# Closer-spaced last norms, one feed-forward step per event, and a norm's scale and shift folded into the output product

## The reference, cut to what matters

```python
# second attention block, on x = layernorm(h)
combined = mh_out + kv_ret                     # two retrievals from running sums
mu = combined.mean(-1, keepdims=True)
var = combined.var(-1, keepdims=True)
lnx = (combined - mu) / jnp.sqrt(var + 1e-05) * ln_g + ln_b
return x + (lnx @ out_w + out_b)
# second feed-forward block, on features = layernorm(h); 6 experts, the best 2 are kept
rh = jax.nn.relu(features @ router_w1 + router_b1)
expert_logits = jax.nn.softmax(rh @ router_w2 + router_b2, axis=-1)
top_w, top_i = jax.lax.top_k(expert_logits, TOP_K)
routing_weights = jax.nn.softmax(top_w, axis=-1)
h1 = jax.nn.relu(jnp.einsum('bsd,edh->bseh', features, expert_w1) + expert_b1)
h2 = jax.nn.relu(jnp.einsum('bseh,ehf->bsef', h1, expert_w2) + expert_b2)
expert_out = jnp.einsum('bsef,efo->bseo', h2, expert_w3) + expert_b3
# the chosen two, weighted and added
```

## Time and profile before

| | us |
|---|---|
| median of 3 runs | 1428.61 |
| lowest and highest | 1426.0, 1433.91 |
| the profiled execution, own time | 1428.26 |
| its span, first to last instruction | 1426.3 |

### The profile page before, as it was taken

The page is one execution under the profiler, slowest core; times in us unless marked ns, Lnnn a source line. Parts: engine busy times, 40 slices in busy tenths (PEclk is TensorE's granted clock), DMA queues, the critical chain, the costliest instruction groups (busy, mean ns, idle before and its releaser), DMA issues.

```text
span 1426.3 us, 26246 instructions
## 1 busy us (share of the span) xinstructions
PE 1163.8 (82%) x9789; PEld 741.6 (52%) x9789; DVE 810.9 (57%) x1763; ACT 643.1 (45%) x1370; POOL 552.9 (39%) x1126
## 2 busy tenths in 40 slices
PE   4599999999999999999999963603287865785688
PEld 3355666656666666666666642201265654653443
DVE  3445555655566566565666522225798989835432
ACT  0326555555554555555455421301546546443444
POOL 3201445734545545455454443178512224212100
PEclk9769999999999999999999986955676777677889
DMA  3100000000000000000000011112000000000000
GB/s 81 20 1 2 2 2 2 5 5 2 4 2 2 2 2 2 2 2 2 2 3 2 2 30 60 62 16 21 7 1 1 1 1 1 12 1 6 11 11 17
DMA packets 31290, 14.59 MB, mean 10 GB/s; under 512 B 27570, under 2 KB 28562, under 8 KB 31165
## 3 DMA queue, kind: packets, MB, share of 16 engines
q1 hardware_dynamic: 26557, 11.01, 3.2%
q0 software_dynamic: 4608, 1.91, 1.5%
HBM read 6.52 MB, written 7.27 MB: 10 GB/s over the span
## 4 chain that ended last, share of the span: by engine, by line
PE 74%; DVE 15%; issue 4%; POOL 2%; ACT 2%; DMA 2%; SPq 0%; DVEq 0%; POOLq 0%; ACTq 0%
PE psum L753 20%; PE psum L734 10%; PE psum L662 8%; PE psum L725 7%; PE psum L709 3%; PE psum L1001 3%; PE psum L647 2%; PE psum L981 2%; PE psum L572 1%; DVE arena L1971 1%; PE psum L991 1%; PE psum L1016 1%; PE psum L667 1%; PE psum L850 1%; PE psum L804 1%
## 5 line engine op out<-in xcount | busy, mean ns | idle before, releaser
L1436 ACT ACTIVATE arena<-psum 125x500 f32<-125x500 f32 x576 | 306.8, 585 | 338.8 <-PE psum L734 338.8
L1777 DVE TENSOR_REDUCE arena<-psum 125x1 f32<-125x500 f32 x384 | 242.6, 673 | 203.1 <-PE psum L662 202.9
L662 PE MATMUL psum<-arena 32*125 32x500 f32 (+1 forms) x1536 | 324.5, 520 | 0.6 <-ACT arena L1427 0.6
L753 PE MATMUL psum<-arena,XN 125*64 125x250 f32 x2304 | 307.9, 388 | 0.2 <-ACT arena L1436 0.2
L734 PE MATMUL psum<-arena 32*125 32x250 f32 x2304 | 291.7, 370 | 0.0
L734 PEld LDWEIGHTS psum<-arena 32*125 32x125 f32 x2304 | 214.6, 183 | 11.8 <-issue 1.0
L753 PEld LDWEIGHTS psum<-arena,XN 125*64 125x64 f32 x2304 | 140.3, 136 | 121.2 <-issue 78.6
L1780 DVE TENSOR_REDUCE arena<-psum 125x2 f32<-125x500 f32 x192 | 121.4, 674 | 71.9 <-PE psum L662 71.9
L1193 POOL TENSOR_TENSOR lnst<-lnst,mhalf 125x12 f32<-125x12 f32 x14 | 32.2, 2297 | 256.9 <-DVE lnst L1756 256.9
L662 PEld LDWEIGHTS psum<-arena 32*125 32x125 f32 x1536 | 128.1, 184 | 4.1 <-issue 2.4
L725 PE MATMUL psum<-arena,onesb 3*125 3x500 bf16 x576 | 122.4, 422 | 1.4 <-DMA arena<-arena 1.4
(11 more groups left out here) (337 smaller groups left out, 1951.3 us busy)
## 6 DMA issues: line engine op xcount, KB each, us to landing
arena<-arena SPq DMA_DIRECT2D x192, 1.5 KB
expert_in<-XN SPq DMA_DIRECT2D x8, 256.0 KB, 4.8
arena<-expert_in SPq DMA_DIRECT2D x4, 512.0 KB, 5.1
expert_out<-arena SPq DMA_DIRECT2D x4, 512.0 KB, 2.6
out<-H SPq DMA_DIRECT2D x16, 93.8 KB
expert_in<-XN,slot_in POOLq DMA_INDIRECT x48, 2.5
XN<-expert_out,slot_out POOLq DMA_INDIRECT x48, 3.9
arena<-in_L_ffn_w SPq DMA_DIRECT2D x2, 256.0 KB
```

Source lines behind the costliest of these rows:

```text
L662: last = pe.matmul(ps[0:R, at_:at_ + hi - lo], QH[row:row + 32, b, g, j * R:(j + 1) * R], KH[row:row + 32, b, g, lo:hi], start=True, stop= ...
L753: last = pe.matmul(ctx_bank[64 * h2:64 * h2 + 64, 0:THIRD], XN[:, p, c, a, :], PR[:, x % 4, h2, i * THIRD:(i + 1) * THIRD], start=(c == 0) ...
L1436: act.activation(PR[:, x % 4, h2, :], st_bank[(2 * x + h2) % 3][0:R, 0:2 * THIRD], ACT.Exp)\
L1777: dve.reduce_max(MX[:, q % 2, 0, 2 * h2 + tile:2 * h2 + tile + 1], ps[0:R, 0:2 * THIRD], AX)\
```

## The change

Three things. (1) The list of events: norm and head events get a written place for each quarter (`norm_at`, `gate_at`), `gates` is split in two events (`weighed` for the DVE's `route` and ACT's last exponential; `gates` for the PE's turn and ACT's copies, one x later), and from x = 23 on each x has exactly one step. (2) `ln_g` is multiplied into the rows of `out_w` once, `ln_b @ out_w` is worked out once by a matmul and added to `out_b`, and GpSimd's two operations at `normalize` go. (3) With it, `ln_g` and `ln_b` are loaded as columns (four DMAs) where they were loaded as broadcast rows (two DMAs).

The diff, cut to its core:

```diff
-        ROOM, EARLY, PER = 16, True, 2
         steps1 = [(p, th, ep) for p in range(NP) for th in range(2) for ep in range(3)]
...
-        def ffn_events(x):
...
+        ROOM, FIRST, PER = 16, 23, 1
+        norm_at = {0: (8, 9, 10, 11, 12, 13, 14, 16), 1: (14, 15, 16, 17, 18, 19, 20, 22),
+                   2: (20, 21, 22, 23, 24, 25, 26, 28), 3: (26, 27, 28, 29, 30, 31, 32, 34)}
+        gate_at = {0: 19, 1: 23, 2: 29, 3: 35}
+        todo = [("step", k) for k in range(len(steps1) + 3)]
...
             for p in range(NP):
-                k = x - NJ * (p + 1) - 2
-                if 0 <= k <= 11 and k not in (3, 9, 10):
-                    events.append((("centre", "variance", "normalize", "", "transpose", "product",
-                                    "centre", "variance", "normalize", "", "", "transpose")[k], 2 + k // 6, p))
+                for n, name in enumerate((("centre", 2), ("variance", 2), ("normalize", 2), ("transpose", 2),
+                                          ("product", 0), ("centre", 3), ("variance", 3), ("transpose", 3))):
+                    if norm_at[p][n] == x:
+                        events.append((*name, p))
+            for p in range(NP):
+                if 0 <= x - gate_at[p] <= 3:
+                    events.append((("router", "logit", "weighed", "gates")[x - gate_at[p]], p))
...
-            if EARLY:
-                ffn_events(x)
-        ffn_events(None)
+            for _ in range(PER if x >= FIRST else 0):
+                k = todo[0][1]
+                if x > gate_at[steps1[min(k, len(steps1) - 1)][0]] + 3:
+                    events.append(todo.pop(0))
+        events += todo
...
+                   (W["lng"][r, :], t["L1_attn_ln_g"].unsqueeze(1)),
+                   (W["lnb"][r, :], t["L1_attn_ln_b"].unsqueeze(1)),
...
             def product(p):
 
+                pe.wait_ge(S["out_scaled"], 1)
...
+            pe.wait_ge(S["shift_rows"], 1)
+            ps, done = take(pe, "out_bias")
+            pe.matmul(ps[0:R, 0:128], QF[:, 0, 0:R], W["outw"], start=True, stop=True).then_inc(done, 1)
...
-                    transposes(x, xn_tile, event[2], S["lnx"] if x == 2 else S[f"normed{x}"])
+                    transposes(x, xn_tile, event[2], S[f"normed{x}"])
...
-                pool.tensor_tensor(pairs(H, p), pairs(H, p), rows(bias[0:R, OB:OB + D], 2 * NJ), ALU.add)\
+                if p == 0:
+                    pool.wait_ge(S["out_bias"], 1)
+                pool.tensor_tensor(pairs(H, p).rearrange("r (j a) d -> r j (a d)", a=2),
+                                   pairs(H, p).rearrange("r (j a) d -> r j (a d)", a=2),
+                                   rows(bias[0:R, OBX:OBX + 128], NJ), ALU.add)\
                     .then_inc(S["h_pre"], 1)
...
-                elif kind == "normalize" and x == 2:
-
-                    p = event[2]
-                    pool.wait_ge(S["normed2"], p + 1)
-                    link(pool.tensor_tensor(pairs(XN, p), pairs(XN, p), rows(bias[0:R, LNG:LNG + D], 12), ALU.mult))
-                    pool.tensor_tensor(pairs(XN, p), pairs(XN, p), rows(bias[0:R, LNB:LNB + D], 12), ALU.add)\
-                        .then_inc(S["lnx"], 1)
...
+            act.wait_ge(S["dma_weights"], 16 * len(wd))
+            act.activation(QF[:, 0, 0:R], ones[:, 0:R], ACT.Copy, scale=W["lnb"]).then_inc(S["shift_rows"], 1)
+            k = jobs["out_bias"]
+            act.wait_ge(full[k % 8], k // 8 + 1)
+            act.activation(W["outw"], W["outw"], ACT.Copy, scale=W["lng"]).then_inc(S["out_scaled"], 1)
...
+            ps, done = filled(dve, "out_bias")
+            link(dve.tensor_tensor(bias[0:R, OBX:OBX + 128].rearrange("r (a d) -> r a d", a=2),
+                                   ps[0:R, 0:128].rearrange("r (a d) -> r a d", a=2),
+                                   rows(bias[0:R, OB:OB + D], 2), ALU.add))
...
-                elif kind == "gates":
+                elif kind == "weighed":
                     route(x)
```

More of the change, by code:

```diff
@@ L44 @@
 RS = 1.0 / np.sqrt(float(PP))
-GB, CVB, KSB, GTB, AOB, LNG, LNB, OB, RB2, WD = (
-    0, 8, 264, 392, 394, 658, 722, 786, 850, 856)
+GB, CVB, KSB, GTB, AOB, OB, RB2, WD, OBX = (
+    0, 8, 264, 392, 394, 658, 722, 728, 733)
 NBIAS = 861
@@ L259, in build @@
             "cosines", "prod", "qf_ready", "state", "h_pre", "lnx",
-            "route1", "route1_ex", "route1_pad", "select", "stored")
+            "route1", "route1_ex", "route1_pad", "select", "shift_rows", "out_bias", "out_scaled", "stored")
         gathered = [S["gathered0"], S["gathered1"], S["gathered2"], S["gathered3"]]
@@ L324, in build @@
         mx, im, pos, sums, kept, sl, sx, tx, sy = (r1[:, i, :] for i in range(9))
-        ROOM, EARLY, PER = 16, True, 2
         steps1 = [(p, th, ep) for p in range(NP) for th in range(2) for ep in range(3)]
-        head1 = [(kind, p) for p in range(NP) for kind in ("router", "logit", "gates")]
-        body1 = [("step", k) for k in range(len(steps1) + 3)]
-        given = []
-        def ffn_events(x):
[L336 to L361, removed]
+        ROOM, FIRST, PER = 16, 23, 1
[3 more added lines that the diff above has]
+        todo = [("step", k) for k in range(len(steps1) + 3)]
         events = [("gathered", 0), ("centre", 1, 0), ("variance", 1, 0), ("gathered", 1), ("centre", 1, 1),
@@ L366, in build @@
                   ("cosines", 0), ("chunk", 0)]
-        for x in range(NT + 14):
+        for x in range(NT + 16):
             p, k = divmod(x, NJ)
@@ L547, in build @@
                 wd.append((bias[:, at_:at_ + n], t["L1_attn_" + name].partition_broadcast(128)))
-        for at_, name, n in ((GB, "L0_ffn_gate_b", 8), (LNG, "L1_attn_ln_g", 64), (LNB, "L1_attn_ln_b", 64),
-                             (OB, "L1_attn_out_b", 64), (RB2, "L1_ffn_router_b2", 6)):
+        for at_, name, n in ((GB, "L0_ffn_gate_b", 8), (OB, "L1_attn_out_b", 64), (RB2, "L1_ffn_router_b2", 6)):
             wd.append((bias[:, at_:at_ + n], t[name].partition_broadcast(128)))
@@ L1592, in softmaxes, with last_softmax, gate_tiles @@
                 act.activation(g1[:, 3, :], g1[:, 2, :], ACT.Exp).then_inc(S["route1_ex"], 1)
-            def gate_tiles(p):
+            def last_softmax(p):
                 act.wait_ge(S["route1"], 3 * p + 3)
                 act.activation(g1[:, 5, :], g1[:, 4, :], ACT.Exp).then_inc(S["route1_ex"], 1)
+            def gate_tiles(p):
                 if p == 0:
@@ L1662, in _ @@
                     softmaxes(x)
+                elif kind == "weighed":
+                    last_softmax(x)
                 elif kind == "gates":
@@ L2083, in added @@
                 dve.tensor_tensor(v, v, ps[0:R, 0:3 * 128], ALU.add).then_inc(done, 1)
+            ps, done = filled(dve, "out_bias")
+            link(dve.tensor_tensor(bias[0:R, OBX:OBX + 128].rearrange("r (a d) -> r a d", a=2),
+                                   ps[0:R, 0:128].rearrange("r (a d) -> r a d", a=2),
+                                   rows(bias[0:R, OB:OB + D], 2), ALU.add))
+            dve.sem_inc(S["out_bias"], 1)
+            dve.sem_inc(done, 1)
             for event in events:
```

2 lines of the change are left out of this document (1 added, 1 removed).

## The result

The changed kernel takes 1382.4 us (median of four runs, 1377.86 to 1385.0) against 1427.81 for the kernel before, measured beside it: a ratio of 0.9671, 95% interval 0.9633 to 0.971, which is 41 to 52 us less. The profiled execution took 1382.21, with a span of 1380.3.

A forecast was written before the change was run, and what follows sets the result against it. The DVE's list was taken to bound the last stage's first half, PE waits in a serial chain its second. 33.4 + 2.5 + 9.6 - 7 = 38.5 off 1428.3 gave 1390 us; range 1381 to 1409 for 8 in 10.

The forecast's parts named there:

- my own case: Whole kernel: the main forecast of 1390 us, with its own range 1384 to 1399 and chance 0.57.
- term 2: `logit` and first layers behind PE waits run at a higher clock: -2.5 us, bounds 0 and -4.6.
- term 4: x = 23 to 39: the new list brings PE waits at `gates` of its own, +7 us, bounds 2 and 22.
- term 3: Before the first step: less GpSimd work beside the DVE, 6.3, and DVE waits filled, 3.3; together -9.6 us.
- The six waits go: Last stage, `logit` and `gates` events: steps fill the PE's six waits, -33.4 us.
- At no cost: `out_bias` work hides in the 41.59 us wait for gathered rows; two more SP DMAs are covered by 24 us.
- more than that: Rival: no new wait and the full clock, 47.6 us gained, 1381; chance 0.12.
- The waits move in rather than go: Rival: DVE gate products stop, banks stay taken, the PE stops at the eighth; gain only 23, 1405; chance 0.25.
- Slower: Rival: one step per x goes round serially, 2.9 us more per step, 49 over 17 steps, 1434; chance 0.03.
- No difference: Rival: last third bound by summed DVE and PE work, a new wait takes what the DVE gets back, 1428; chance 0.03.
- the marks that I named: Profile signs: no quarter 1 to 3 wait over 3 us, PE above 85% busy, clock above 0.9, first step near 1253.

The follow-up runs named there:

- the fold alone: Kernel before the change, old list of events kept, with only the norm's scale and shift folded into out_w and out_b: 1420.49 us, ratio 0.9938.
- filled waits: Kernel before the change, with idle matmuls given to the PE in five long waits at `logit` and `gates`: 1423.71 us, ratio 0.996.
- the twin: Changed kernel with two GpSimd operations of the removed shape put back at the same four places, on data nobody needs: 1384.36 us, ratio 0.9676.
- the second profile: Profile of the changed kernel run once more without any edit, for the spread between executions: 1381.15 us, ratio 0.9666.
- the step first: Changed kernel with the step ahead of the norm and head pieces in each x: 1391.16 us; with `gates` of quarters 1 and 2 also later, 1386.04.
- the version with `gates` joined: Changed kernel with `route` one x later, in the same x as `gates`: 1403.42 us, ratio 0.9815.

## Why the prediction came out as it did: the mechanism held, the clock term failed

The mechanism was right: six waits of the PE filled with steps, few new ones, and two operations of GpSimd fewer beside the DVE's chunks. The forecast was a gain of 38.5 and 1390 us; it is 45 us by the medians, 46 by the spans, and 1382.4 lies below the 1384 to 1399 of my own case. The step that failed is term 2, the clock, which I put at 2.5 and which measured 7.8; term 4, the new waits, was too large, 4.4 for 7. Whether term 3 was too small is not settled. Taken in the order of the prediction:

1. *The six waits go, -33.4:* right. The new list alone gives nearly the whole gain; the fold alone leaves 31.8 of them.
2. *The clock, -2.5:* this step failed in size; it is about 7.8. I had counted two `logit` and three first layers, 4.6, and taken back half. Missed were the `gates` matmuls themselves (1.51 for 0.86), the second layers, and the first step. The kernel before, behind `gates` of quarter 2 (its L969 at 1350.77 is in the earlier trace rows):

```profile
1352.21 1.62 PE L981 MATMUL psum<-XT,arena 64*128 64x375 f32 x4
1353.62 1.35 PE L991 MATMUL psum<-arena 64*128 64x375 f32 x4
...
1356.37 0.90 PE L981 MATMUL psum<-XT,arena 64*128 64x375 f32 x4
```

   From `gates` to the next step but one that is 5.6, in the other two quarters 5.2 and 5.9; the changed kernel takes 3.7 (1304.42 to 1308.13, and 1332.14 to 1335.80). Three times makes 16.6 - 11.1 = 5.5, the two `logit` 2.4, the first step 5.96 (1261.00 to 1266.96) for 3.55 in the fold alone, 2.4. The changed kernel gives 2.5 back behind its wait of 2.82 (1270.51 to 1279.86 for 6.6, less the 0.24). 5.5 + 2.4 + 2.4 - 2.5 = 7.8. That the clock has this price was tested: filled waits gave 7.0, where the rows above give 5.5 + 2.4 = 7.9 for the places that they touch. The first step was not tested.
3. *Before the first step, -9.6:* right in kind. It is 13.9 in one profile and 12.2 in the other (303.2 - 293.1 + 2.1), but 11.1 and 9.4 against the 300.4 of the kernel with filled waits, whose list is the old one. The medians leave as much: 45.4 and 48.6 gained, less the 37.6 of the last part, are 8 to 11, an estimate from these numbers. The GpSimd part, 6.3 in the sum, is 3.4 to 6.5 by the twin. The fold alone gives 3.4 to 6.2 there, 1.8 of it behind `gates` of quarter 0 (5.20 to the first step for 6.95), where its PE is back at full clock sooner. Chunk of quarter 0: 2.7 predicted, 2.45 seen. The part of the order, taken as 3.3, is 303.2 - (298.0 - 2.1) = 7.3, above its bound of 5.5, or 4.5 from 300.4, within it; 1.3 of it is again behind `gates`. I had looked at waits of the DVE alone. The PE too waited at `logit` and `gates` of quarter 0, 3.60 at 1240.22 and 5.42 at 1254.05, which the earlier trace rows leaves out; in the changed kernel these are none and 0.73. How much of that counts was not taken apart.
4. *New waits, +7:* 4.4. The one at `gates` of quarter 1 was predicted as 2.5 from a sum of the DVE's work (9.6 - 7.1) and is 2.82; that of quarter 2 as 1 and is 1.35. The 2 for ACT's squares was too much here, though that wait is real: it came up as the 2.88 of `gates` one x later.
5. *At no cost:* as said. SP's last weight load is at 64.06 and its next DMA at 92.78.

The last part adds up: 33.4 - 4.4 = 29.0 of waits and 7.8 of clock are 36.8 of the 37.6 measured; predicted were 33.4 - 7 + 2.5 = 28.9. With 9.4 to 13.9 ahead of it for 9.6, the two parts give 47.0 to 51.5 for 38.5. The parts ahead of the transpose, which the change does not touch, took 2.7 and 5.5 more than in the profile before, so that the spans differ by 47.1 and 46.0. That is near the rival *more than that*, 47.6. But its condition, no new wait, did not hold, and it had 4.6 for the clock: that its number fits is luck, a clock term above even its 4.6 making up for most of the 4.4 of waits.

The rivals. *The waits move in rather than go* (1405) did not come true. Two of the lists tried come out near its number, 1401 with two steps in an x and 1403 with `route` and `gates` in one x, but not by its mechanism: their long waits are at `gates`, for `route`, and not for a bank. *Slower*, by a serial round of each step, is refuted: a plain step takes 2.9 (1305.21 to 1308.13), as before, and no wait at L980 is over 0.24. *No difference* is refuted by the ratio. Of the marks that I named most held: the longest wait left is the 2.82 at `gates` of quarter 1, the PE is busy for 95% from the first step to the last turn, the last `gates` stands ahead of step 15, the chunk has two stretched operations instead of four, that of 1207 us none (L1963 takes 0.69 there). The granted clock is 0.97 from 1270 to 1380 us, but 0.64 from 1271.3 to 1276. The first L960 came at 1254.65 for 1253, with the 6.5 us of the late start in it, and at 1253.59 in the second profile. The first wait of L725 (L703 here) for a DMA ends at 95.56 and, in the second profile, at 91.05, for 89.98 before, later by about as much as the first norm.

## What to carry to other kernels

Where an engine stands idle at the same few events, ask first what independent work of its own stands behind them in its list; moving it there is worth the wait and what the PE loses by coming back at half clock, here 7 to 8 us on 33. When a list is in order on all engines, count the events between a result and its reader on every engine that the chain passes: here one x between `route` and `gates` is worth 21 us and a second one nothing. Profile one list more than once before you read a few us out of a part: here one part repeated to 0.1 us and another only to 4. Two edits that shorten the same wait do not add up; time each alone before you share out the gain.

## What was not expected of the hardware

- The price of an idle PE goes on well behind the wait. After 6.97 us of idle time the next 5.6 us of matmuls did the work of 3.7. With work of no use in the waits the same instructions ran at full clock. After the 2.82 us of the changed kernel the next 9.1 did the work of 6.6; that this wait is the cause is not shown, since the same three groups slow down alike with the step first, where no wait stands ahead of them.
- An operation with a single input also stretches beside GpSimd: L2037, a TENSOR_SCALAR of 125x12, took 1.24 at 1279.21 in the version with `gates` joined, where the like take 0.17. GpSimd's L1178, on 125x768, had started at 1278.94 and took 1.47; it was done at 1280.41 and L2037 at 1280.45.
- The first 60 us differ between executions. The first line here is of the kernel before, the second of the changed one; the matmuls are the same:

```profile
36.92 1.73 PE L572 MATMUL psum<-arena 96*96 96x250 f32 x10
```

```profile
36.94 2.98 PE L550 MATMUL psum<-arena 96*96 96x250 f32 x10
```

  The first norm then starts at 57.8 to 60.3 in nine of the profiled executions and at 64.4 to 64.5 in four, the changed kernel in both groups. The granted clock from 30 to 64 us is shown as 0.86 in the one that is fast there and 1.00 in the slow one, so that column does not explain it, nor does it bear out the half clock that I took for the cause before the second timing, and I leave it open. It moves the first norm by 4 to 7 us and the transpose after the expert stage by 3 to 6 us, 0.4%, in any single profile: parts of a profile should be compared from a common event on, and not by their place in the span.
